# Shared-expert phase of a fused transformer kernel: turn pace, place of the logits, bank of the expert places

## What is computed

```
def _L1_ffn_ref(u, g_shared, W1_s, ..., centroids):
    h_s = _experts_mlp(u, g_shared, W1_s, b1_s, W2_s, b2_s).sum(axis=-2)      # 2 shared experts, all tokens
    scores = jax.nn.sigmoid(u @ centroids)                                    # 8 routed experts
    gpk, i_topk = jax.lax.top_k(scores, 2)
    gk = gpk / scores.sum(axis=-1, keepdims=True)
    routed_all = _experts_mlp(u, g_routed, W1_r, b1_r, W2_r, b2_r)
    h_r = (gk[..., None] * take_along_axis(routed_all, i_topk)).sum(axis=-2)
    return u + h_s + h_r
x = x + 0.5 * _L1_ffn_ref(_layernorm(x), ...)
```

## Time and profile before

| | us |
|---|---|
| median of 3 runs | 2860.8 (2859.31 to 2874.13) |
| profiled execution, its time | 2870.94 |
| its span | 2869.2 |
| first expert stage, shared phase | from about 1228 to 1505 |
| second expert stage, shared phase | from about 2227 to 2501 |
| PE, VectorE, ScalarE, POOL busy, of the span | 81%, 71%, 48%, 42% |

### The profile page before, as it was taken

The page is one execution under the profiler, slowest core; times in us unless marked ns, Lnnn a source line. Parts: engine busy times, 40 slices in busy tenths (PEclk is TensorE's granted clock), DMA queues, the critical chain, the costliest instruction groups (busy, mean ns, idle before and its releaser), DMA issues. The chain is left out here.

```text
span 2869.2 us, 51222 instructions
## 1 busy us (share of the span) xinstructions
PE 2330.8 (81%) x14828; PEld 1656.7 (58%) x14828; DVE 2025.6 (71%) x5474; ACT 1377.8 (48%) x2654; POOL 1212.7 (42%) x1060
## 2 busy tenths in 40 slices
PE   5569999999999896778899998088888788898980
PEld 5435455444444554666677776066777676777760
DVE  7666666666666665778777776588888787776664
ACT  4204454455444544666756665032222667666650
POOL 3342211221131132528774555145655387645550
PEclk9759899999998997988999999599999988999995
DMA  2031122121112213401135665500000111356646
GB/s 64 15 45 25 28 34 34 25 35 31 31 28 31 36 24 88 163 34 41 43 122 180 219 218 170 136 1 0 0 0 0 39 41 43 120 200 212 212 161 176
DMA packets 140258, 222.67 MB, mean 78 GB/s; under 512 B 20958, under 2 KB 100624, under 8 KB 129515
## 3 DMA queue, kind: packets, MB, share of 16 engines
q1 hardware_dynamic: 121835, 185.46, 23.6%
q0 software_dynamic: 18176, 34.14, 3.5%
HBM read 136.75 MB, written 57.32 MB: 68 GB/s over the span
## 5 line engine op out<-in xcount | busy, mean ns | idle before, releaser
L950 DVE TENSOR_REDUCE attn_rowmax<-psum 128x1 f32<-128x512 f32 (+3 forms) x748 | 457.8, 637 | 297.4 <-PE psum L788 295.5
L732 ACT ACTIVATE attn_probs<-psum 128x512 f32<-128x512 f32 (+1 forms) x704 | 387.2, 560 | 493.3 <-PE psum L851 484.9
L786 PE MATMUL psum<-attn_ks,attn_qs 72*128 72x512 bf16 (+3 forms) x1088 | 314.5, 325 | 38.2 <-DVE attn_rowmax L950 31.4
L849 PE MATMUL psum<-attn_qs,attn_ks 75*128 75x512 bf16 (+3 forms) x1024 | 290.9, 316 | 36.3 <-issue 25.7
L788 PE MATMUL psum<-attn_mask_qk,attn_ident_b 128*128 128x128 bf16 x1088 | 223.7, 231 | 0.0
L1274 POOL DMA_INDIRECT experts_answers<-ffn1b_y_rows,ffn1b_out_row x156 | 154.4, 990 | 151.3 <-ACT ffn1b_y_rows L1344 111.0
L1274 POOL DMA_INDIRECT experts_answers<-ffn1a_y_rows,ffn1a_out_row x156 | 154.8, 992 | 147.1 <-ACT ffn1a_y_rows L1344 109.3
L849 PEld LDWEIGHTS psum<-attn_qs,attn_ks 75*128 75x128 bf16 x1024 | 101.8, 100 | 193.1 <-ACT attn_probs L732 94.4
L648 POOL TENSOR_TENSOR attn_rstd<-attn_var_eps,minus_half 128x4 f32<-128x4 f32 x18 | 18.3, 1018 | 445.3 <-DVE attn_var_eps L927 445.3
L851 PE MATMUL psum<-attn_mask_kq,attn_ident_b 128*128 128x128 bf16 x1024 | 205.2, 226 | 0.0
L1824 POOL TENSOR_TENSOR gla_state<-gla_state,gla_qT 128x512 f32<-128x512 f32 x128 | 160.0, 1270 | 106.8 <-DVE gla_state L2023 106.8
(11 more groups left out here) (421 smaller groups left out, 6355.4 us busy)
## 6 DMA issues: line engine op xcount, KB each, us to landing
ffn1a_w_ring<-experts_packed SPq DMA_DIRECT2D x39, 1026.5 KB, 5.1
ffn1b_w_ring<-experts_packed SPq DMA_DIRECT2D x39, 1026.5 KB, 5.1
attn_qs<-attn_qparts SPq DMA_DIRECT2D x216, 64.0 KB
attn_ks<-attn_kparts SPq DMA_DIRECT2D x216, 64.0 KB
ffn1a_x_in<-experts_slots SPq DMA_DIRECT2D x39, 264.0 KB, 4.8
ffn1b_x_in<-experts_slots SPq DMA_DIRECT2D x39, 264.0 KB, 4.7
ffn1a_h<-experts_answers SPq DMA_DIRECT2D x16, 512.0 KB, 5.5
ffn1b_h<-experts_answers SPq DMA_DIRECT2D x16, 512.0 KB, 5.4
```

The lines of the kernel that those rows point to most:

```text
L732: act.activation(probs[:, j % RING, 0:n], ps_exp[j % 2][:, 0:n], ACT.Exp, scale=SCALE).then_inc(exp_ready, 1)
L786: pe.matmul(out, qs[k][0:K_QK, 4 * g + hh, qt * P:(qt + 1) * P], ks[k][0:K_QK, 4 * g + hh, 0:n_keys], start=True, stop=False)
L849: pe.matmul(out, ks[k][:, 4 * g + hh, kt * P:(kt + 1) * P], qs[k][:, 4 * g + hh, kt * P:N], start=True, stop=False)
L950: dve.tensor_reduce(rowmax[:, NT - 1 - w, h:h + len(heads)], score_bank(n, j)[:, 0:len(heads) * width_of(w)].rearrange("p (a c) -> p a c", ...
```

## The change

It edits the tables that place the side jobs, splits the shared bank, and adapts the semaphores. Nothing is computed in another way.

- **Turns**: tile r is turned at unit r - 1 + r // 3 (-1, 0, 1, 3, 4, 5, 7, 8, 9, 11, 12, 13, 15, 16, 17, 19), which is three tiles in four units; before it was (3 (r - 1) + 1) // 2 (-1, 0, 2, 3, 5, 6, 8, 9, 11, 12, 14, 15, 17, 18, 20, 21), two in three. Normalise stays one unit ahead of the turn, prepare two.
- **Logits** come two units after the turn in place of one, and have bank 5 for themselves; their scaling opens VectorE's next unit, ahead of best two and split, where it followed the split of the same unit.
- **Exponent and best two** come 3 and 4 units after the turn of the group's second tile (2 and 3 before), **rank** 5 units after it, rounded up to an even unit: 6, 8, 10, 14, 16, 18, 22, 24 (before: 5, 8, 11, 14, 17, 20, 23, 26).
- **Ranks and totals** move to bank 7, which they share with the turned outputs, in even units between the turn-outs of the odd ones; `out_used` counts the uses.
- At the start prepare(0) comes before moments 1 and 2.

```diff
-    turn_at = {r: (3 * (r - 1) + 1) // 2 if r else -1 for r in range(S)}
+    turn_at = {r: r - 1 + r // 3 for r in range(S)}
     tile_turned = {u: r for r, u in turn_at.items()}
-    logits_at = {turn_at[r] + 1: r for r in range(S)}
-    exp_at = {turn_at[2 * g + 1] + 2: g for g in range(GROUPS)}
-    best_at = {turn_at[2 * g + 1] + 3: g for g in range(GROUPS)}
-    rank_at = {turn_at[2 * g + 1] + 5: g for g in range(GROUPS)}
+    logits_at = {turn_at[r] + 2: r for r in range(S)}
+    exp_at = {turn_at[2 * g + 1] + 3: g for g in range(GROUPS)}
+    best_at = {turn_at[2 * g + 1] + 4: g for g in range(GROUPS)}
+    even = lambda u: u + u % 2
+    rank_at = {even(turn_at[2 * g + 1] + 5): g for g in range(GROUPS)}
     moments_at = {r - 3: r for r in range(3, S)}
-    prepare_at = {turn_at[r] - 2: r for r in range(2, S)}
+    prepare_at = {turn_at[r] - 2: r for r in range(3, S)}
     normalise_at = {turn_at[r] - 1: r for r in range(2, S)}
-    totals_at = max(rank_at) + 1
...
+    totals_at = max(rank_at) + 2
+    turn_out_at = {E_S * i + E_S + 1: i for i in range(S)}
+    out_bank = sorted([(u, "turn", i) for u, i in turn_out_at.items()] + [(u, "rank", g) for u, g in rank_at.items()]
+                      + [(totals_at, "totals", 0)])
...
-        ps_misc = m.psum[:, 5, :]
+        ps_logit = m.psum[:, 5, 0:G * E_R].rearrange("p (t e) -> p t e", e=E_R)
...
                 def rank(g):
-                    misc_free(misc_count["rank", g])
+                    out_free("rank", g)
                     pe.wait_ge(hot_ready, g + 1)
-                    out = ps_misc[:, 0:2 * G * E_R].rearrange("p (t e) -> p t e", e=E_R)
+                    out = ps_out[:, 0:2 * G * E_R].rearrange("p (t e) -> p t e", e=E_R)
...
                 def turn_out(q):
                     pe.wait_ge(yT_ready, q + 1)
-                    if q >= 1:
-                        if q <= S:
-                            pe.wait_ge(x_done, q)
-                        else:
-                            pe.wait_ge(row_ready, q - S)
+                    if q < S:
+                        out_free("turn", q)
+                    elif q == S:
+                        pe.wait_ge(out_used, len(out_bank))
+                    else:
+                        pe.wait_ge(row_ready, q - S)
...
-                for r in range(3):
+                moments(0)
+                prepare(0)
+                for r in range(1, 3):
                     moments(r)
...
-                prepare(0)
+                low_input(0)
                 prepare(1)
-                low_input(0)
+                prepare(2)
...
                 for u in range(UNITS):
+                    if u - 1 in logits_at:
+                        scale_logits(logits_at[u - 1])
                     if u in best_at:
                         best_two(best_at[u])
                     split(u)
                     if u < SHARED:
                         if u in tile_turned:
                             low_input(tile_turned[u])
-                        if u in logits_at:
-                            scale_logits(logits_at[u])
```

More of the change, by code:

```diff
@@ L1412, in rank @@
                     pe.matmul(out, ex.ones[:, :], along(counts[:, g % 2, :], 1, 2 * G), start=False,
-                              stop=True).then_inc(misc_psum, 1)
+                              stop=True).then_inc(rank_psum, 1)
                 def totals():
-                    misc_free(misc_count["totals", 0])
-                    pe.matmul(ps_misc[:, 0:E_R], ex.ones[:, :], counts[:, GROUPS % 2, :], start=True,
-                              stop=True).then_inc(misc_psum, 1)
+                    out_free("totals", 0)
+                    pe.matmul(ps_out[:, 0:E_R], ex.ones[:, :], counts[:, GROUPS % 2, :], start=True,
+                              stop=True).then_inc(rank_psum, 1)
                 def up(u):
@@ L1554, in best_two @@
                     if g >= 1:
-                        dve.wait_ge(misc_psum, misc_count["rank", g - 1] + 1)
+                        dve.wait_ge(rank_psum, g)
                     for k in range(2):
@@ L1689, in _ @@
                             prepare(prepare_at[u])
-                        if u % 2 == 1 and u >= 3:
-                            residual((u - 3) // 2)
+                        if u in turn_out_at:
+                            residual(turn_out_at[u])
                         if u == SHARED - 1:
```

52 lines of the change are left out of this document (26 added, 26 removed).

## The result

| | before | after |
|---|---|---|
| median | 2862.06 us (4 runs, 2859.31 to 2874.13) | 2975.76 us (4 runs, 2971.48 to 2979.78) |
| ratio after / before | | 1.0387, 95% interval 1.0351 to 1.0424 |
| profiled execution, its time / its span | 2870.94 / 2869.2 us | 2979.78 / 2978.0 us |

The changed kernel is 113.7 us slower; 2977 us had been forecast. It leaves out by how much the stages of different kernels begin earlier or later for other reasons (the first stage between 1219.30 and 1234.72 us).

What follows compares the result with a forecast made beforehand. POOL's scatter chain, closed by the ring of six slots, was taken as the bound. 4.9 + 49.3 + 3.8 = 58 us a stage, 116 for two, gave 2987 profiled, less 10 for the median: 2977 us, range 2905 to 3010.

Steps and rivals of the forecast that it cites:

- part 3: Shared phase: ScalarE's closing slot wait precedes gelus feeding the same scatter; group 0 to 5 takes 184.5 us, +49.3 a stage.
- The releases: Scatters landing free ScalarE's next normalise, 13.0 us (even tile) or 25.4 us (odd tile) after the group's first scatter.
- step 2 to 3: Scatter group 2 to 3: tile 11 released at 25.4, gelu(14) 33.2, split to 38.5, a little for PE: 40.5 us.
- The start: VectorE sets the first scatter; rank(0) a unit later adds 7.1 us, prepare(0) first gives back about 1.6: +4.9 us.
- The end: From group 5's start PE ends after POOL; first routed turn 84.3 us behind where it was 80.5: +3.8 us.
- Logits in a bank of their own: PE's 18.9 us of waits for logits scaling go, costed at nothing because ScalarE's scatter waits cover them.
- Places in the bank of the turned outputs: Ranks wait for residuals, turn-outs for places; bounds nothing to 25 us a stage, taken as nothing by ScalarE's wait.
- PE's clock: After a stall PE runs at 1.2 GHz, up to 2.8 us more a block; 1.5 us counted once, in step 2 to 3.
- half of it: Rival: rows come sooner, POOL starves in every second group only; 25 us a stage, 2911 us, chance 0.12.
- As written: Rival: gain on PE, POOL never waits and starts no later; 10 us a stage faster, 2841 us, chance 0.03.
- nothing: Rival: POOL never waits, but its first scatter comes later; 2851 us, chance 0.06.
- More: Rival: PE's slow clock lies on the path, nine stalls of 2.8 us, 25 a stage; 3027 us, chance 0.07.

Runs made afterwards that it cites:

- The two ring sizes: Changed kernel with seven or eight slots for normalised tiles instead of six: 2864.7 us (0.9992) with seven, 2851.1 us (0.9959) with eight.
- the old pace: Changed kernel with the turn table of the kernel before (two tiles in three units), all else as changed: 2919.4 us, ratio 1.0198.
- early ranks rounded up: Kernel before with new banks, eight slots, prepare(0) first, ranks in units 4, 8, 10, 14, 16, 20, 22, 26: 2845.8 us, ratio 0.9923.
- after with eight slots: Changed kernel with eight slots for normalised tiles instead of six, order of every engine unchanged: 2851.1 us, ratio 0.9959.
- before with eight: Kernel before with eight slots for normalised tiles instead of six: 2843.3 us, ratio 0.9923.

## Why the prediction was right, step by step

**The mechanism** was the one named: the wait for scatters moved ahead of the gelus that feed the same scatters. The two ring sizes bear it out from one side, the old pace from another: there only the groups that the order puts behind both waits become slow, and one more late in the phase.

**The steps of part 3**, each from first scatter to first scatter:

| step | forecast | measured |
|---|---|---|
| group 0 to 1 | 39 | 36.5 |
| 1 to 2 | 37 | 35.8 |
| 2 to 3 | 40.5 | 41.1 |
| 3 to 4 | 36 | 32.5 |
| 4 to 5 | 32 | 31.9 |
| sum | 184.5 | 177.75 |

The sum is 6.75 us too long, and its terms are off by more than that in both directions. The releases are too long. That of an odd tile was taken as 25.4 us from the kernel before; now it is 21.7 (1301.67 to 1323.40), because while ScalarE waits VectorE falls idle, and then a scatter with its issue takes 1.28 us in place of about 1.5: of the fifteen scatters behind the first, seven took 1.10 to 1.71 us before, and all take 0.97 or 0.98 now. A duration was carried over from a busy stretch into an idle one. The even tile has 11.5 us (1301.67 to 1313.20) in place of 13.0. Over the five steps the releases are 14 us too long, and the way from the release to the next scatter is 7 us too short. Half of these 7 lies in step 2 to 3, where gelu(14) waits 3.00 us for PE, a term that had only "a little":

```profile
1407.65 2.79 ACT L1321 ACTIVATE ffn1a_h<-psum,ffn1a_w_shared 128x512 f32<-128x512 f32 x4 [3.00 <-PE psum L1435]
```

**The start** was forecast at +4.9 us; from the stage's own beginning to the first scatter it went from 61.3 to 68.4 us, +7.2. The step was right in kind and 2.3 us short. **The end** was forecast at +3.8 us; from the start of group 5 to the first routed turn it is 87.3 us (1479.42 to 1566.75) where 84.3 were forecast, so +6.8. As foreseen PE now ends the phase, and its routed turn follows the last shared matmul without a gap:

```profile
1566.51 0.40 PE L1450 MATMUL psum<-ffn1a_hh,ffn1a_w_shared 128*128 128x512 f32 x1
1566.75 0.60 PE L1393 MATMUL psum<-ident,ffn1a_x_in 128*128 128x128 f32 x4
```

So a stage is 7.2 + 42.6 + 6.8 = 56.6 us longer in place of 58. The forecast for the total is within 2 us, but partly by chance: -6.75 in the middle and +5.3 at the two ends offset one another. So did two terms outside the phases: the profiled execution came at 2979.78 where 2987 was forecast, since the rest of the kernel was 5.9 us shorter; and that execution lay only 4 us above the median, where the forecast had taken off 10.

**Logits in a bank of their own, costed at nothing:** the price was right, the reason was not. The prediction says that these waits go. They fell from 18.9 to 8.8 us, and in the kernel with the new banks, the old place of the logits and early ranks rounded up they are 17.0 us. All seven waits of the kernel before are of one tile's logits for the scaling of the tile before, and these two still share a place in the new bank. By the order, what the change gives back comes from the later logits and the earlier scaling; it is not seen in the time, even where slots hardly bind (after with eight slots, 10.8 us of slot waits, is 7.8 us slower than before with eight). The rule of the Trainium skill that was set against this, with 37.8 us to gain, does not decide here, since these waits are for the scaling of the tile before, in the same place of the bank.

**Places in the bank of the turned outputs, costed at nothing:** right for the kernel as changed (PE waited 4.6 us in three waits for residuals), and for the reason that ranks stand on even units. The upper bound of 25 us was no fancy, though: with ranks on odd units PE waited 15.0 to 18.6 us a stage for places.

**PE's clock:** it fell as foretold, 0.67 to 0.77 in the stalled stretches against 0.85 to 0.93. What it cost was not separated from the 57 us. With eight slots the stalls go and the clock is back at 0.83 to 0.97, so that run says nothing of its price inside a stall. In step 2 to 3, whose terms leave under 1 us where the prediction speaks of 1.5, it lay on the path: between 1402.50 and 1405.30 the granted clock is 0.50, that is 1.2 GHz, a matmul takes 0.63 us in place of 0.40, and behind this block gelu(14) waits its 3.00 us.

**What was wrong in the list of signs:** POOL's scatters were to stay at 190.6 us with issue; they are 172.6 (135.2 + 37.4). Waits for rows of 8 to 16 us were to stand ahead of groups 1 to 5; they stand by that name ahead of groups 3 to 6 (11.8, 12.3, 11.7 and 5.8 us), and ahead of groups 1 and 2 as a wait for the variance of an inverse. The largest slot waits were to be those of tiles 6, 8, 10 and 12; they are those of tiles 8, 6, 12 and 14 (19.7, 19.1, 16.0 and 15.8 us), and tile 10 has 9.2. "The title" in the prediction is the change's short description, "turns at two tiles per three units"; its code sets three in four, and the old-pace run shows what two in three would have given: 2919 us. That answers a sentence of the prediction, that at two in three the closing wait would not move. It moves for every second group, and half of the loss stays; the prediction overlooked that ranks a unit later do what turns a unit earlier do.

**The rivals:** "half of it" (2911) is almost exactly what the old pace gives, so it was the right price for a different table. "As written" and "nothing" needed rows in time; with eight slots the time is 2851 us, the number that "nothing" gave. "More", through the clock, did not come.

The 7.8 us by which the changed order with eight slots is slower than the old one with eight can be followed in the traces. Its first scatter comes 68.4 us after the stage's beginning (1226.81 to 1295.24) against 61.3 (1224.04 to 1285.36), so 7.1 us later. The seven steps from there to the last group are 5.6 us shorter (173.5 against 179.1), 3.7 of them in the first step, and from the start of the last group to the first routed turn it is 2.3 us longer (31.0 against 28.7). That makes 3.8 us in the first stage; the second has 3.6, by the same three parts.

What stays open: the share of PE's slow clock in the loss, and which of the later side jobs makes the half that the pace does not; by the order it is the ranks, but no run moves them alone.

## What to carry to other kernels

When a side job moves earlier on an engine that works in order, ask of every wait in it what stands behind it, and whether the one who ends the wait is fed by that. If so, the wait closes a ring, and its price is not its own length: in the kernel before, 37 us of such waits cost some 7 us a stage (lengths 551.1 and 536.9); in the changed one 84 us go with 57 more, and one buffer more takes that away. Price such a ring by walking once round it with durations from the trace, but take them from stretches whose neighbours are as idle as they will be then. And when a user moves into another's PSUM bank, look at which unit each falls in: two uses in one unit put 15 to 18 us of waits on PE in a stage here, in alternating units under 5 us. Before counting on a bank of its own, read who the waits are for: here they were for the same use, one tile before.

## What was unexpected of the hardware

**An indirect DMA on POOL takes 0.97 us beside an idle VectorE and up to 1.72 us when it meets VectorE's fp32 subtraction.** At the end of the phase of the kernel after the two alternate (rows of both engines in order of time):

```profile
1549.23 0.69 DVE L1645 CAST ffn1a_hh<-ffn1a_h 128x1024 fp32r<-128x1024 f32 x1
1549.99 1.23 DVE L1647 TENSOR_TENSOR ffn1a_hl<-ffn1a_h,ffn1a_hh 128x1024 fp32r<-128x1024 f32 x1
1550.46 1.60 POOL L1266 DMA_INDIRECT experts_slots<-ffn1a_xs,ffn1a_rows  x1 [0.30 <-issue]
1551.13 0.69 DVE L1645 CAST ffn1a_hh<-ffn1a_h 128x1024 fp32r<-128x1024 f32 x1
1551.89 1.23 DVE L1647 TENSOR_TENSOR ffn1a_hl<-ffn1a_h,ffn1a_hh 128x1024 fp32r<-128x1024 f32 x1
1552.36 1.60 POOL L1266 DMA_INDIRECT experts_slots<-ffn1a_xs,ffn1a_rows  x1 [0.31 <-issue]
```

Sorted by what VectorE did at the time, the 128 scatters of stage a in the kernel before are 12 beside an idle VectorE with a mean of 0.98 us, 67 that overlap the subtraction by more than 0.08 us with 1.38 (up to 1.72), and 49 beside other work with 1.00; in the kernel after they are 52, 31 and 45. That is why a scatter became shorter on average (1195 to 1056 ns) in a kernel that became slower, and the run without the subtraction shows the cause of the larger part. The Trainium skill, "SBUF — State Buffer" (Who interferes with whom), says that a VectorE instruction with two SBUF inputs contends with a GpSimd instruction that reads SBUF, and names VectorE as a cause of late descriptors for DMAs issued from GpSimd. The trace agrees: the subtraction has two SBUF inputs and goes with scatters longer by up to 0.75 us (1.72 against 0.97), and once it is left out, with all casts still there, the mean is 1.03 us. The same section holds, of a probe of its own, that `tensor_copy` stalled such DMAs and `tensor_tensor` did not; here the measurement decides, and `tensor_tensor` does: the 20 scatters of stage a in the kernel before that overlap it and no cast take 1.60 us on average. The cast, which has one SBUF input, does too, but less often: without the subtraction 44 scatters of stage a overlap one, with a mean of 1.12 us and up to 1.75. So in a kernel whose bound is POOL's indirect DMAs, 21 us a stage depend on what VectorE does beside them.
